# A third split projection in the attention pipeline, with the rows of the next chunk normalised on ScalarE

## The reference, cut to what matters

```python
h1 = adaln(x, t, norm1_w, norm1_b)          # layernorm(x) * (1 + scale) + shift
x = mha(h1, h1, ...attn1...) + x            # 16 heads of 64, softmax over 64 keys
h2 = adaln(x, t, norm2_w, norm2_b)
x = mha(h2, context, ...attn2...) + x
h3 = adaln(x, t, norm3_w, norm3_b)
x = glu_ff(h3, ff_w1, ff_b1, ff_w2, ff_b2) + x
...
x = x + L0_xcond(layernorm(x), cond[:, None, :], ctx)
x = x + L0_ffn(layernorm(x), wqkv, w1, w2)   # 8 experts, top 2 by router logits
```

## Time and profile before

| | us |
|---|---|
| median of three runs | 2146.03 (2144.26 to 2146.51) |
| the profiled execution | 2165.7 |
| its span | 2163.8 |
| TensorE busy in the span | 2056.7 |
| ScalarE, VectorE, GpSimd busy | 1403.1, 1328.3, 1065.3 |

### The profile page before, as it was taken

The page is one execution under the profiler, slowest core; times in us unless marked ns, Lnnn a source line. Parts: engine busy times, 40 slices in busy tenths (PEclk is TensorE's granted clock), DMA queues, the critical chain, the costliest instruction groups (busy, mean ns, idle before and its releaser), DMA issues. The chain is left out here.

```text
span 2163.8 us, 38718 instructions
## 1 busy us (share of the span) xinstructions
PE 2056.7 (95%) x11132; PEld 1349.0 (62%) x11132; DVE 1328.3 (61%) x3405; ACT 1403.1 (65%) x2665; POOL 1065.3 (49%) x1198
## 2 busy tenths in 40 slices
PE   6899999999999999999999999999999897798996
PEld 5455556555556656555555565656565576788995
DVE  4554657676767666666666676666657654455565
ACT  4566666666767676767676767676766656565663
POOL 1443444636363737373737373736454263555653
PEclk9999999999999999999999999999999999999998
DMA  4111111111111111111211112121113121112266
GB/s 131 46 33 34 49 35 50 45 49 44 53 44 48 44 48 46 50 57 38 58 39 53 52 41 53 39 53 44 44 50 110 45 57 48 51 53 68 61 187 204
DMA packets 136322, 127.36 MB, mean 59 GB/s; under 512 B 14665, under 2 KB 110569, under 8 KB 136234
## 3 DMA queue, kind: packets, MB, share of 16 engines
q1 hardware_dynamic: 127466, 109.11, 18.1%
q0 software_dynamic: 8768, 17.20, 2.4%
HBM read 86.63 MB, written 40.67 MB: 59 GB/s over the span
## 5 line engine op out<-in xcount | busy, mean ns | idle before, releaser
L1860 POOL TENSOR_TENSOR pr<-pr,sm 128x512 f32<-128x512 f32 x256 | 277.4, 1097 | 492.4 <-DVE sm L1414 492.4
L1090 ACT ACTIVATE kp<-ps 128x512 f32<-128x512 f32 x512 | 298.4, 600 | 182.4 <-PE ps L281 178.1
L816 PE MATMUL ps<-tt,V 128*128 128x512 f32 x768 | 381.2, 594 | 3.5 <-ACT tt L1090 3.5
L1404 DVE TENSOR_REDUCE mx<-ps 128x8 f32<-128x512 f32 x256 | 176.8, 691 | 312.8 <-PE ps L765 312.8
L1090 ACT ACTIVATE tt<-ps 128x512 f32<-128x512 f32 x512 | 274.9, 590 | 40.3 <-PE ps L795 40.2
L765 PE MATMUL ps<-kp,hf 128*64 128x256 f32 x2048 | 277.0, 392 | 7.2 <-DVE pr L1407 3.8
L281 PE MATMUL ps<-cT,M 128*128 128x512 f32 x768 | 260.5, 462 | 0.0
L765 PEld LDWEIGHTS ps<-kp,hf 128*64 128x64 f32 x2048 | 124.4, 136 | 197.7 <-DVE pr L1407 139.2
L281 PE MATMUL ps<-hk,M 128*128 128x512 f32 x768 | 244.5, 441 | 1.9 <-DVE hk L1468 1.9
L1090 ACT ACTIVATE pt<-ps 128x512 f32<-128x512 f32 x256 | 153.4, 599 | 141.9 <-PE ps L777 139.4
L917 PE MATMUL ps<-xT,wt 128*128 128x128 f32 (+1 forms) x1728 | 224.5, 281 | 17.2 <-DVE ux L1674 7.6
(11 more groups left out here) (228 smaller groups left out, 3584.7 us busy)
## 6 DMA issues: line engine op xcount, KB each, us to landing
mod<-emb_s SPq DMA_DIRECT2D x96, 256.0 KB, 4.3
xr<-rows_s SPq DMA_DIRECT2D x144, 66.0 KB
cb<-y_s SPq DMA_DIRECT2D x32, 256.0 KB, 5.3
x_in<-in_x_dram SPq DMA_DIRECT2D x16, 256.0 KB, 4.4
xn_s<-x_in SPq DMA_DIRECT2D x16, 256.0 KB, 2.0
res<-xn_s SPq DMA_DIRECT2D x16, 256.0 KB, 2.7
c_in<-in_ctx_dram SPq DMA_DIRECT2D x16, 256.0 KB, 4.8
y_s<-res SPq DMA_DIRECT2D x16, 256.0 KB, 2.0
```

The source lines that it names most:

```text
L816: mm = nc.tensor.matmul(psO[:], Vw[a][:, g * HG + head_at(h), :], tt[:, h, :], start=(g == 0 and h == 0), stop=ends)
L1090: return nc.scalar.activation(o, i, ACT.Copy)
L1404: nc.vector.tensor_reduce(mx[:, p % 2, :], heads(psS[p % 2][:]), AX_X, ALU.max).then_inc(max_done, 1)
L1860: tensor(v, v, sm[:, p, :].unsqueeze(2).broadcast_to([P, HG, 64]), ALU.mult).then_inc(prob_done, 1)
```

## The change

- `RU` gets unit 1. `V0`, the unsplit weights of attention 1, now holds only the four heads a unit that stay unsplit; a new `R1` of the same size as what V0 gives up holds the split ones. `whole(u)` picks the unsplit weights. `split_seq` counts three split units a round.
- GpSimd's three `split` calls, ScalarE's `last_split` and VectorE's `last_rest` run in slot 2 as well. There `last_split` comes after the fourth key copy (h = 3) and `last_rest` at h = 4, behind `ln_lo` and `ln1`.
- `ln_norm` of the outer layernorm goes from VectorE to ScalarE: `norm1`, four ACTIVATEs with a bias and a scale per row, at hook 1 of slot 2, ahead of the second key copy. The bias, minus mean times inverse deviation, is one more product in GpSimd's `ln1_rstd`.
- VectorE's `router_dot` moves from hook 4 to 5, behind `ln1` and `last_rest`; GpSimd's `router_mul` from 2 to 1.
- At startup `norm1(0)` stands in ScalarE's stream ahead of the last four setup tiles.

```diff
-            RU = (3, 0)
-            R0 = sa("R0", [P, 2, HR, D], F32R)
+            RU = (3, 0, 1)
+            R0, R1 = (sa(f"R{u}", [P, 2, HR, D], F32R) for u in range(2))
...
+        def whole(u):
+
+            return V0[:, u] if u < 2 else V1[:, (u - 2) * HG:(u - 1) * HG]
...
-                    mm = nc.tensor.matmul(psO[:], Vw[a][:, g * HG + head_at(h), :], tt[:, h, :], start=(g == 0 and h == 0), stop=ends)
+                    mm = nc.tensor.matmul(psO[:], whole(u)[:, h if u in RU else head_at(h), :], tt[:, h, :], start=(g == 0 and h == 0), stop=ends)
...
+            def norm1(c):
+                act.wait_ge(rstd[0], 6 * c + 2)
+                for t in range(NT):
+                    op = nc.scalar.activation(x_in[:, t, :], x_in[:, t, :], ACT.Identity, bias=lv[0][:, 3, t:t + 1], scale=lv[0][:, 7, t:t + 1])
+                op.then_inc(nrm[0], 1)
...
-                         2: ((3, 2, lambda c: ln_hi(c, 2)), (5, 2, lambda c: glu_act(c, 0)), (6, 2, lambda c: glu_split(c, 0)),
+                         2: ((1, -1, norm1), (3, 2, lambda c: ln_hi(c, 2)), (5, 2, lambda c: glu_act(c, 0)), (6, 2, lambda c: glu_split(c, 0)),
...
-                    if h == 1 and last and lu in RU:
+                    if h == (3 if u == 2 else 1) and last and lu in RU:
                         last_split(li, lu)
...
             def ln1(c):
 
-                dve.wait_ge(rstd[0], 5 * c + 5)
-                ln_norm(0, x_in, x_in)
+                dve.wait_ge(rstd[0], 6 * c + 6)
                 dve.wait_ge(nrm[0], c + 1)
...
-                         2: ((2, 3, router_sum), (4, 3, router_dot), (3, 2, lambda c: ln_lo(c, 2)), (4, -1, ln1), (6, 2, lambda c: glu_mul(c, 0)), (7, 2, lambda c: glu_split_lo(c, 0)), (8, -1, lambda c: ln_lo(c, 0)), (8, 3, top_first)),
+                         2: ((2, 3, router_sum), (3, 2, lambda c: ln_lo(c, 2)), (4, -1, ln1), (5, 3, router_dot), (6, 2, lambda c: glu_mul(c, 0)), (7, 2, lambda c: glu_split_lo(c, 0)), (8, -1, lambda c: ln_lo(c, 0)), (8, 3, top_first)),
...
-                    if h == 2 and last and lu in RU:
+                    if h == (4 if u == 2 else 2) and last and lu in RU:
                         last_rest(li, lu)
...
                 tensor(v[:, 7, :], v[:, 6, :], half[:], ALU.pow).then_inc(rstd[0], 1)
-                pool.wait_ge(rstd[0], 5 * c + 1)
+                pool.wait_ge(rstd[0], 6 * c + 1)
+                tensor(v[:, 3, :], v[:, 4, :], v[:, 7, :], ALU.mult).then_inc(rstd[0], 1)
...
-                         2: ((2, 3, router_mul), (4, 3, router_out)),
+                         2: ((1, 3, router_mul), (4, 3, router_out)),
```

More of the change, by code:

```diff
@@ L130, in sa @@
                 return sb(name, shape, dt, phase_a)
-            M0, V0 = sa("M0", [P, 2, H, D], F32R), sa("V0", [P, H, D])
+            M0, V0 = sa("M0", [P, 2, H, D], F32R), sa("V0", [P, 2, HF, D])
             hk = sa("hk", [P, 2, CT], F32R)
@@ L136, in pixart_block_moe @@
             h1 = sa("h1", [P, NT, D])
-            RU = (3, 0)
-            R0 = sa("R0", [P, 2, HR, D], F32R)
+            RU = (3, 0, 1)
+            R0, R1 = (sa(f"R{u}", [P, 2, HR, D], F32R) for u in range(2))
             M1, V1 = sa("M1", [P, 2, H, D], F32R), sa("V1", [P, H, D])
             R3 = sa("R3", [P, 2, HR, D], F32R)
-            Mw, Vw, Vr = [M0, M1], [V0, V1], {0: R0, 3: R3}
+            Mw, Vw, Vr = [M0, M1], [V0, V1], {0: R0, 1: R1, 3: R3}
             W1 = sa("W1", [P, 2, 2 * DFF], F32R)
@@ L365, in split_seq @@
             if first(i):
-                return 0
+                return u
             if isinstance(i, int) and i == NC:
-                return 2 * NC - 1
-            return 2 * i - (u == 0)
+                return 3 * NC - 1
+            return 3 * i - 1 + u if u < 2 else 3 * i + 1
         def rounds(engine, body):
@@ L1110, in setup_copy @@
                         at, src = 2 * (g % 2), ps[:].rearrange("p (a two b) -> p a two b", a=2, two=2)
-                        copy(Vw[a][:, 8 * (g // 2) + g % 2:8 * (g // 2) + 8:4, :], src[:, :, 0, :])
+                        copy(whole(unit)[:, at:at + 2, :], src[:, :, 0, :])
                         op = copy(Vr[unit][:, 0, at:at + 2, :], src[:, :, 1, :])
@@ L1338, in slot @@
                 fill(i, u, HG)
-            setup(0, N1)
+            setup(0, N1 - H // 4)
+            norm1(0)
+            setup(N1 - H // 4, N1)
             ln_hi(0, 0)
@@ L1431, in ln_stats @@
                 dve.wait_ge(stat[k], z + 7)
-                nc.vector.tensor_scalar(v[:, 4, :], v[:, 0, :], 0.5, None, ALU.mult).then_inc(stat[k], 1)
+                nc.vector.tensor_scalar(v[:, 4, :], v[:, 0, :], -0.5 if k == 0 else 0.5, None, ALU.mult).then_inc(stat[k], 1)
                 nc.vector.scalar_tensor_tensor(v[:, 3, :], v[:, 1, :], D / 4.0, v[:, 1, :], ALU.mult, ALU.mult).then_inc(stat[k], 1)
@@ L1880, in ln1_rstd @@
                 tensor(v[:, 7, :], v[:, 6, :], half[:], ALU.pow).then_inc(rstd[0], 1)
-                pool.wait_ge(rstd[0], 5 * c + 1)
+                pool.wait_ge(rstd[0], 6 * c + 1)
+                tensor(v[:, 3, :], v[:, 4, :], v[:, 7, :], ALU.mult).then_inc(rstd[0], 1)
                 tensor(v[:, 8, :], v[:, 5, :], v[:, 7, :], ALU.mult).then_inc(rstd[0], 1)
-                pool.wait_ge(rstd[0], 5 * c + 2)
+                pool.wait_ge(rstd[0], 6 * c + 3)
                 tensor(v[:, 9, :], v[:, 8, :], v[:, 7, :], ALU.mult).then_inc(rstd[0], 1)
-                pool.wait_ge(rstd[0], 5 * c + 3)
+                pool.wait_ge(rstd[0], 6 * c + 4)
                 tensor(v[:, 10, :], v[:, 9, :], eps[:], ALU.add).then_inc(rstd[0], 1)
-                pool.wait_ge(rstd[0], 5 * c + 4)
+                pool.wait_ge(rstd[0], 6 * c + 5)
                 tensor(v[:, 11, :], v[:, 10, :], half[:], ALU.pow).then_inc(rstd[0], 1)
```

## The result

The changed kernel takes 2152.55 us (median of 7 runs, 2151.55 to 2155.5) against 2145.09 (7 runs, 2143.25 to 2146.51) for the kernel before on the same chip: a ratio of 1.0037, with a 95% interval of 1.0027 to 1.0046. It is 7.5 us slower. The profiled execution took 2153.05 us, its span is 2151.3. The profiled execution of the kernel before was a long one, 2165.7 us against a median of 2145.09; its extra time lies behind 1824.93 us, so its trace is compared with the others only up to there.

The account below looks back on a forecast made before the run. TensorE's own stream was taken to bound the loop. The split's -10.9 us and the norm's +16.3 sum to +5.4, on a median of 2146.0 giving 2151.4 us; range 2141 to 2158.

Parts of the forecast that it names:

- Term 1: TensorE, slot 2: splitting four of unit 1's heads saves 0.68 us a chunk over 16 chunks, -10.9 us.
- Rival D: TensorE's split: the triple costs as much as the product, leaving only the stall, 2162.3 us; chance 0.02.
- Term 2: ScalarE, slot 2: four norms ahead of ln_hi delay glu_up, stalling TensorE 1.28 us a round, +16.3 us.
- Rival A: ScalarE's norms: cheaper, one surcharge of about 0.09 instead of two, 1.1 us in all, 2146.2 us; chance 0.28.
- Rival B: TensorE at glu_up: the stall never arrives, room exceeds 1.1 us, split alone remains, 2135.1 us; chance 0.06.
- The round: Loop round of four slots: 105.2 + 1.28 - 0.68 = 105.8 us.
- happen once; I take zero: Setup and startup: unit 1's weight address, two copies for one, and the startup norm cost zero, bound 1.02 us.
- rival C: VectorE, slot 2: ln1 and last_rest slow beside GpSimd's probabilities, losing over 2.8 us together, 2164 us; chance 0.19.
- the cover: VectorE, slot 2: some 2.8 us between last_rest's end and TensorE's head 4 hide VectorE's added work.
- A sign that was wrong: TensorE, slot 2: glu_up's weight load would idle about 1.3 us for VectorE's h, 12 or 13 times.

Follow-up runs that it names:

- e9: Changed kernel with the norms behind ScalarE's copy ln_hi (as e2) and the first GLU product a head later (as e6): 2127.76 us.
- e2: Changed kernel with norm1 moved in ScalarE's stream from hook 1 to hook 3 of slot 2, behind ln_hi: 2137.47 us.
- e5: Kernel before with the norms on ScalarE at hook 1 of slot 2, without the third split: 2159.77 us.
- e7: Changed kernel with the norm as a copy with a scale per row, the bias left out: 2151.82 us (one run).
- e3: Changed kernel with the four norms replaced by plain copies of the same size at the same place: 2141.14 us.
- e6: Changed kernel with the first GLU product a head later in TensorE's slot 2 (h = 4 instead of 3): 2131.11 us.
- e12: The same kernel as e6, run once more: 2130.15 us.
- e8: Changed kernel with GpSimd's six split operations of unit 1 shrunk from 128x512 to 128x8: 2153.85 us.
- e4: Changed kernel with each norm of 128 columns cut in two of 64, eight ACTIVATEs at the same place: 2191.65 us.
- e1: Changed kernel with the four norms given back to VectorE at the head of ln1, third split kept: 2141.39 us.
- e10: e6 with four more ScalarE instructions a round in slot 1, the last pair's copy cut into five pieces: 2131.7 us.

## Why the prediction was right

The forecast was 2151.4, +5.4 us; measured +7.5. The sign, the mechanism and both terms hold.

- **Term 1, the split.** Forecast -0.68 us a chunk, measured 3.92 against 4.57, -0.65. e9 and e2 have this term without the stall: -8.3 and -7.3 us over thirteen rounds (e2 with 0.95 us of waiting for a DMA), where 13 x 0.65 are 8.5. Rival D is out.
- **Term 2, the norm.** Forecast 0.49 us each and 1.5 in the queue; measured 0.491 and 1.53. Forecast room 0.22, measured 0.21 (1.53 - 1.32). Forecast stall 1.28, measured 1.32; over thirteen rounds e5 gives 17.0 against 16.3. Rival A needed one surcharge instead of two; e7 and e3 show both. Rival B needed over 1.1 us of room.
- **The round.** Forecast 105.8, measured 105.86.
- **Where 2.1 us were mis-sized: "happen once; I take zero".** In the loop the difference to before grows by 0.65 us a round, from +0.75 us in round 2 to +9.14 in round 15, and at the first row of the expert tiles it is +7.4 (1758.54 and 1765.97). The growth is near the forecast (0.60 a round, 0.30 less in the first: 7.5 in all, measured 8.4). But in round 2 the sum should have stood at -1.4, since rounds 0 and 1 had their splits and no stall; it stood at +0.75. The 2.1 us are lost up to the first turn of `htm` (+1.43 against -0.68). 0.41 of them are there when round 0's projection begins (90.00 and 90.41). That is the scatter of the startup: the same kernel twice, e6 and e12, begins at 91.33 and 90.30. Most of the rest is the norm of the next chunk in round 0. Before, VectorE had made it early and TensorE's transposes of h came at once:

```profile
84.03 1.12 DVE L1443 TENSOR_SCALAR x_in<-x_in,lv 128x128 f32<-128x128 f32 x4 [3.05 <-POOL lv L1888]
```
```profile
90.00 3.70 PE L816 MATMUL ps<-tt,V 128*128 128x512 f32 x8 [1.17 <-ACT tt L1090]
93.53 0.60 PE L822 MATMUL ps<-ident,h 128*128 128x128 f32 x4
```

In the changed kernel it is queued on ScalarE behind the copies of `tt`, so that `ln1` begins 7 us later (91.98 against 85.18), beside GpSimd's split, and TensorE waits for it. ScalarE, VectorE and TensorE:

```profile
88.27 2.08 ACT L1094 ACTIVATE tt<-ps 128x512 f32<-128x512 f32 x4 [0.21 <-PE ps L799]
90.24 1.64 ACT L1174 ACTIVATE x_in<-x_in,lv 128x128 f32<-128x128 f32 x4
```
```profile
91.98 2.51 DVE L1471 SCALAR_TENSOR_TENSOR h<-x_in,lv,mod 128x128 f32<-128x128 f32 x4 [10.60 <-ACT x_in L1174]
```
```profile
90.41 3.70 PE L820 MATMUL ps<-tt,V 128*128 128x512 f32 x8 [1.17 <-ACT tt L1094]
95.37 0.63 PE L826 MATMUL ps<-ident,h 128*128 128x128 f32 x4 [1.26 <-DVE h L1474]
```

From the projection to the transposes it is 4.96 us against 3.53, 1.43 lost. The late norm alone does not do it. In e8, with the norm in the same place and GpSimd's split cut down, `ln1` begins as late and the stretch is 3.58 us. VectorE, then TensorE:

```profile
91.89 1.14 DVE L1471 SCALAR_TENSOR_TENSOR h<-x_in,lv,mod 128x128 f32<-128x128 f32 x4 [10.60 <-ACT x_in L1174]
```
```profile
90.32 3.70 PE L820 MATMUL ps<-tt,V 128*128 128x512 f32 x8 [1.17 <-ACT tt L1094]
93.90 0.63 PE L826 MATMUL ps<-ident,h 128*128 128x128 f32 x4
```

In e5, with no third split, it is 3.59. And in e3, whose four copies take 0.7 us less of ScalarE's queue, it is 4.97, as `ln1` takes 3.26 us. So it takes both: ScalarE's queue brings `ln1` beside GpSimd's split, and there its four operations take 2.51 us in place of 1.14. That is rival C's outcome, slower operations past their cover, in one round. What I had used as the cover was the loop's picture; in round 0 there are no key copies and no GLU between, so the cover isn't there. Nearly all of the remaining 0.27 us is the split itself, which gains only 0.44 in round 0: from the transposes to those of `oT` it is 4.38 us against 4.82.
- **Two misses that cancel.** The loop lost 0.9 us more than the sum has. Behind it the sum has the one split of round 15, -0.68, and the difference fell by 1.7, from +9.14 to +7.43 at the last turn of `htm` (1793.17 and 1800.60). 0.70 of that is the split. The other 1.0 comes with the clock: TensorE waits 3.55 and 2.71 us for the same things in both traces, but the clock is 0.50 from 1704 to 1706 and from 1714 to 1716 before, and from 1714 to 1716 and from 1738 to 1740 in the changed kernel. That these two nearly cancel is luck.
- **Rival C in the loop.** Half of it happened: the four operations of `ln1` lost 1.94 us (3.08 against 1.14), of the 2.1 to 4.7 that C gave to six. The fifth and `last_rest`, at 0.69 and 0.68, lost nothing; GpSimd's work had ended by then, as the prediction held against C. The cover took it, and e8 shows that removing it gains nothing.
- **A sign that was wrong.** I expected the wait to appear as a wait for VectorE's `h`. It is there, 1.09 us eight times between 600 and 1500 us, but put down to "issue". Only VectorE's own row (2.32 behind ScalarE's copy) names the chain. The spacing of starts gave 1.32 us; the bracket gave 1.09.

## What to carry to other kernels

Work moved to an engine that is idle on average costs what it puts ahead of that engine's next result on the path; here four instructions of 0.49 us, a few places too early, turned a gain of 8 us (e2) into a loss of 7. Before moving a step, measure the room of the first consumer behind its new place (here 0.2 us), and if it is short, put the step behind that result, or move the consumer back in its own stream; both gave 104.57 us a round here. Look at the first rounds by themselves: the work that covers a step in the loop may not exist there.

## What the runs showed of the hardware

- TensorE's granted clock fell to 0.50 (1.2 GHz) behind idle time of 2.19 us in seven of twelve rounds of e4 and behind 1.93 us in one, 1.6 us a time, and not after 1.09 us in the changed kernel's loop. Where it fell, the stall of 2.19 us cost 1.7 times its length. Behind the loop, with waits of 2.5 to 3.6 us, it fell at other places from trace to trace, so that a single trace can't tell 1 or 2 us there.
- VectorE's operations on 128x128 slip beside GpSimd's: the one with two full SBUF inputs (`h<-x_in,lv,mod`) has a median of 820 ns in the changed kernel and 345 in e8 and e5. The TENSOR_SCALAR with only one full input was slow as well beside GpSimd's work: 1.02 us for four before, 3.19 in e1. No run takes GpSimd's work away from beside it, so the cause is argued there.
- ScalarE's queue can stand still while the instruction queue moves packets: ten times some 4.7 us in e4, with seven packets across each wait, where the changed kernel has three in that part of a round and no such wait. Four more instructions elsewhere (e10) didn't do it. What sets the number stays open.
- Part of the order's value lay outside the loop: a product moved by one head let expert rows fill a wait in one late round, 4.4 us between two traces, of which some 2.2 by the order and the rest with the clock.
